# Two input quadrants kept on chip, transposed by columns, and projected by rows from there

## What is computed

```python
def layer_0(z):                                   # z is [256, 256, 64]
    n = ln(z)
    a = (n @ W_ap + b_ap) * sigmoid(n @ W_ag + b_ag) * mask[..., None]
    b = (n @ W_bp + b_bp) * sigmoid(n @ W_bg + b_bg) * mask[..., None]
    return z + einsum('ikc,kjc->ijc', a, b) @ W_z + b_z

def layer_1(x):
    n = ln(x)
    left  = sigmoid(n @ left1)  * (n @ left2)
    right = sigmoid(n @ right1) * (n @ right2)
    p = ln(einsum('sre,kre->ske', left, right))
    return x + (p @ out_w) * sigmoid(n @ gate)
```

## Time and profile before

| | us |
|---|---|
| median of 3 runs | 995.39 (992.37 to 997.83) |
| the profiled execution | 993.22 |
| its span | 991.6 |
| TensorE matmul busy | 817.9 |
| VectorE busy | 763.9 |
| ScalarE busy | 635.0 |
| GpSimd busy | 590.0 |

### The profile page before, as it was taken

How to read it: one execution, slowest core, us unless ns; L and a number is a source line. 1 busy time by engine, 2 the same in 40 slices (tenths; PEclk the granted TensorE clock), 3 DMA queues, 4 the chain that set the end, 5 groups by cost and what they waited for, 6 DMA issues and landing times.

```text
span 991.6 us, 26391 instructions
## 1 busy us (share of the span) xinstructions
PE 817.9 (82%) x9820; PEld 786.3 (79%) x9820; DVE 763.9 (77%) x1851; ACT 635.0 (64%) x866; POOL 590.0 (59%) x410
## 2 busy tenths in 40 slices
PE   4654444567999899989899999999999999999865
PEld 3553344467899799989899999898999898989754
DVE  6899999987589958995388888708980897069896
ACT  5698888765667536753266777547763776257664
POOL 7699999987256504660376444405661667068887
PEclk9789999798999999999899999999999999999999
DMA  4455489988789718969665768857982797876675
GB/s 139 117 161 150 131 275 297 342 286 299 256 274 316 226 33 270 307 205 282 235 194 156 241 214 297 325 193 215 296 279 66 216 306 225 291 253 226 212 233 191
DMA packets 173397, 228.75 MB, mean 231 GB/s; under 512 B 11224, under 2 KB 109784, under 8 KB 171224
## 3 DMA queue, kind: packets, MB, share of 16 engines
q1 hardware_dynamic: 172408, 226.96, 71.7%
q10 hardware_dynamic: 864, 0.12, 0.1%
HBM read 134.76 MB, written 92.27 MB: 229 GB/s over the span
## 4 chain that ended last, share of the span: by engine, by line
PE 43%; DVE 20%; DMA 15%; issue 11%; POOL 4%; ACT 3%; SPq 3%; DVEq 0%; POOLq 0%; ACTq 0%
PE bank L1117 18%; PE ps_w L1151 6%; DVE stats L944 6%; PE bank L1097 6%; DMA xin<-in_x_dram 6%; PE bank L1098 5%; DVE split L988 3%; PE ps_t L1136 3%; DMA xt<-xt 3%; DVE xc L981 2%; DMA xin<-x 2%; PE ps_x L1162 2%; DVE var L951 2%; DVE xc L973 2%; DMA chunk<-xcol 2%
## 5 line engine op out<-in xcount | busy, mean ns | idle before, releaser
L660 POOL TENSOR_TENSOR rstd<-var,minus_half 128x8 f32<-128x8 f32 x192 | 343.8, 1791 | 321.4 <-DVE var L951 321.4
L1117 PE MATMUL bank<-rhs,lhs 128*128 128x128 f32 x1536 | 227.6, 281 | 13.5 <-DVE lhs L924 7.5
L1117 PEld LDWEIGHTS bank<-rhs,lhs 128*128 128x128 f32 x1536 | 200.2, 196 | 16.4 <-DVE lhs L924 8.2
L718 ACT ACTIVATE sig<-bank 128x512 f32<-128x512 f32 x256 | 152.0, 602 | 63.5 <-PE bank L1098 61.1
L745 ACT ACTIVATE xt<-ps_x 128x1024 bf16<-128x1024 bf16 x128 | 130.9, 1022 | 60.6 <-PE ps_x L1162 47.1
L1162 PE MATMUL ps_x<-ident_b,split 128*128 128x128 bf16 x1024 | 83.3, 227 | 95.8 <-DVE split L988 95.3
L1162 PEld LDWEIGHTS ps_x<-ident_b,split 128*128 128x128 bf16 x1024 | 67.1, 102 | 107.3 <-DVE split L988 106.0
L981 DVE TENSOR_TENSOR xc<-xc,rstd 128x504 f32<-128x504 f32 (+1 forms) x192 | 137.9, 718 | 16.1 <-POOL xc L674 13.9
L1097 PE MATMUL bank<-w_rhs,chunk 128*128 128x128 bf16 x1024 | 136.9, 228 | 6.5 <-DVE rhs L916 2.7
L1098 PE MATMUL bank<-w_rhs,chunk 128*128 128x128 bf16 x1024 | 136.0, 227 | 0.0
L1097 PE MATMUL bank<-w_lhs,chunk 128*128 128x128 bf16 x928 | 125.8, 227 | 9.4 <-DVE lhs L916 4.4
(11 more groups left out here) (114 smaller groups left out, 1592.3 us busy)
## 6 DMA issues: line engine op xcount, KB each, us to landing
chunk<-xt SPq DMA_DIRECT2D x90, 512.0 KB, 4.5
xt<-xt SPq DMA_DIRECT2D x80, 512.0 KB, 5.4
xin<-in_x_dram SPq DMA_DIRECT2D x128, 256.0 KB, 4.7
x<-xin SPq DMA_DIRECT2D x64, 256.0 KB, 5.1
xin<-x SPq DMA_DIRECT2D x64, 256.0 KB, 4.9
out_dram<-xin SPq DMA_DIRECT2D x64, 256.0 KB, 4.6
spill<-lhs SPq DMA_DIRECT2D x8, 1024.0 KB, 5.4
chunk<-xcol SPq DMA_DIRECT2D x16, 512.0 KB, 5.6
```

The lines of the kernel that those rows point to most:

```text
L660: g.tensor_tensor(rstd[:, m % 2], var[:, m % 2], minus_half[:, :], ALU.pow).then_inc(rooted, 1)
L718: a.activation(sig[:, s], v[:, 0:C, :], ACT.Sigmoid).then_inc(gated, 1)
L1117: last = mm(bank[:, n], operand_of(q // 4, "lhs", kh)[:, c, :], operand["rhs"][:, kh, c, :], start=kh == 0, stop=kh == HALVES - 1)
```

## The change

Chunks 16 to 31 are no longer stored by rows and loaded back. `col_out` keeps quadrant 0 whole in the second half of the left operand's tile (`resident[0]`) and quadrant 2 whole in `quad` (`resident[2]`), 32 KB a partition each, and `project` reads a row of them as 128 elements that lie 128 bfloat16 (256 bytes) apart, where a row chunk has them 16 (32 bytes) apart. `xt_out` and `store_xt` are left out for quadrants 0 and 2; quadrant 2's columns are stored in 8 DMAs of 512 KB (`store_resident`) where there were 16 of 256 KB. Quadrant 3's first eight steps are staged in `chunk`. The schedule has three "last z" ticks where it had six, and steps 51 to 55 stand in the "second half" ticks; contraction 0 starts at tick 59 instead of 62. GpSimd's masks stay at their tick numbers, so those of ticks 59 to 61 now stand in the contraction's first three units, and a unit waits for its own channels' mask only. The spills move with them. At the start the seven `loads` stand in tick 1 and the six `loads_diag` in tick 3, behind the loads of steps 4 and 5. The diff, cut to its core:

```diff
     return layer, op, kind, half, i % GROUPS, i // GROUPS
-DIRECT = CHUNKS
+DIRECT = 2 * CHUNKS
...
         tick("z", m, [m])
-    for m in range(3 * STEPS, Z_LATE - 2):
+    for m in range(3 * STEPS, Z_HALF):
         tick("last z", m)
+    late = dict(zip((0, 2, 3, 5, 6), range(Z_HALF, Z_LATE)))
     for i in range(8):
-        tick("second half", {2: Z_LATE - 2, 5: Z_LATE - 1}.get(i), [48 + 2 * i, 49 + 2 * i], spill=(0, 0, i // 2 - 1) if i in (3, 5, 7) else None)
+        tick("second half", late.get(i), [48 + 2 * i, 49 + 2 * i], spill={5: (0, 0, 0), 7: (0, 0, 1)}.get(i))
     contraction(0, dict(zip((0, 1, 2, 3, 5, 6, 8, 9), range(Z_LATE, 4 * STEPS))),
-                {0: (0, 0, 3), 3: (0, 1, 0), 7: (0, 1, 1), 11: (0, 1, 2), 15: (0, 1, 3)})
+                {1: (0, 0, 2), 2: (0, 0, 3), 4: (0, 1, 0), 7: (0, 1, 1), 11: (0, 1, 2), 15: (0, 1, 3)})
...
     return ticks
-Z_EARLY, Z_LATE = 22, 56
+Z_EARLY, Z_HALF, Z_LATE = 22, 51, 56
...
 VECTOR_MASKS = {0: ("lhs", 1, 2), 1: ("lhs", 0, 2), 2: ("rhs", 0, 2)}
-EARLY = range(DIRECT + GROUPS, DIRECT + GROUPS + 6)
+def by_rows(m):
+    return step(m)[0] == "x" or step(m)[1] == 1
 def load_tick(n):
-    layer, _, kind, half, group, other = chunk_of(FIRST_OF[n])
-    last = 2 * STEPS + STEPS - 1 if n in EARLY else 0
-    if kind == "row":
-        last = STEPS * (QUADRANTS.index(("z" if layer == 0 else "x", half, other)) + 1) - 1
-    else:
-        last = X_BASE - 1
-    stored = TICK_OF[("store", "step", last)]
-    if n in EARLY:
-        return stored + (n - EARLY[0]) // 2
+    stored = TICK_OF[("store", "step", STEPS * (source_of(n) + 1) - 1)]
+    if n < DIRECT + 2:
+        return max(stored, TICK_OF[("store", "step", Z_LATE - 1)])
...
             at[0] += width
-            assert at[0] <= 6144
+            assert at[0] <= P * C
             return scratch[0:rows, at[0] - width:at[0]]
-        staged = [scratch[:, 6144 + 512 * n:6144 + 512 * (n + 1)].bitcast(BF16) for n in range(4)]
+        resident = {0: operand["lhs"][:, 1].rearrange("p c j -> p (c j)").bitcast(BF16),
+                    2: scratch.bitcast(BF16)}
...
         def col_buffer(m):
-            if m < 2 * STEPS:
+            q, c0 = m // STEPS, step(m)[3]
+            if q in resident:
+                return resident[q][:, P * c0:P * (c0 + COLS)]
+            if m < SIG_STAGED:
                 return chunk[:, (m // 2) % 2, P * COLS * (m % 2):P * COLS * (m % 2 + 1)]
-            if m < SIG_STAGED:
-                return staged[m % 4]
             return sig_staged[m % 2]
-        early = [scratch[:, 1024 * n:1024 * (n + 1)].bitcast(BF16) for n in range(len(EARLY))]
...
                 layer, _, kind, half, group, other = chunk_of(FIRST_OF[n])
-                if n in EARLY:
-                    sp.wait_ge(ready, 2)
-                    dst, landed = early[n - EARLY[0]], early_landed[n - EARLY[0]]
+                dst, landed = chunk[:, n % 2], chunk_landed[n % 2]
+                if n < DIRECT + 2:
+                    sp.wait_ge(projected, after(2 * CHUNKS - 1))
+                    for b in range(4):
+                        sp.wait_ge(col_stored[b], 16 * (Z_LATE - 3 * STEPS) // 4)
...
+            def store_resident(m):
+                _, rh, _, c0 = step(m)
+                sp.wait_ge(col_done, after(m))
+                sp.dma_start(xcol_dram[rh, :, c0 - COLS:c0 + COLS, :],
+                             resident[2][:, P * (c0 - COLS):P * (c0 + COLS)].rearrange("p (j r) -> p j r", r=P)
+                             ).then_inc(resident_stored, 16)
...
                 sp.dma_start(dst, src).then_inc(first_loaded, 16)
-            for dst, src in loads:
-                sp.dma_start(dst, src).then_inc(loaded, 16)
-            sp.wait_ge(zeroed, 1)
-            for dst, src in loads_diag:
-                sp.dma_start(dst, src).then_inc(loaded, 16)
...
                         load_x(m)
+                if t == 1:
+                    for dst, src in loads:
+                        sp.dma_start(dst, src).then_inc(loaded, 16)
+                if t == 3:
+                    sp.wait_ge(zeroed, 1)
+                    for dst, src in loads_diag:
+                        sp.dma_start(dst, src).then_inc(loaded, 16)
...
                 for m in due("store", t, "zx"):
-                    if m % 2:
+                    if m % 2 and by_rows(m):
                         store_xt(m)
-                    if 2 * STEPS <= m < X_BASE:
+                    if m % 2 and m // STEPS == 2:
+                        store_resident(m)
+                    if m // STEPS == 3:
...
             def col_out(m):
+                q = m // STEPS
                 act.wait_ge(x_turned, after(m))
-                if m < 2 * STEPS:
+                if q == 1 and m - 4 >= STEPS:
                     act.wait_ge(projected, after(m - 4))
-                elif m < SIG_STAGED:
-                    if m == 2 * STEPS:
-                        act.wait_ge(ready, 2)
-                    if m - 4 >= 2 * STEPS:
-                        act.wait_ge(col_stored[m % 4], 16 * ((m - 4 - 2 * STEPS) // 4 + 1))
-                else:
+                if m == 2 * STEPS:
+                    act.wait_ge(ready, 2)
+                if q == 3 and m < SIG_STAGED:
+                    if m - 4 < 3 * STEPS:
+                        act.wait_ge(projected, after(2 * CHUNKS - 1))
+                    else:
+                        act.wait_ge(col_stored[m % 4], 16 * ((m - 4 - 3 * STEPS) // 4 + 1))
+                if m >= SIG_STAGED:
...
                     if m - 2 >= SIG_STAGED:
-                        act.wait_ge(col_stored[(m - 2) % 4], 16 * ((m - 2 - 2 * STEPS) // 4 + 1))
+                        act.wait_ge(col_stored[(m - 2) % 4], 16 * ((m - 2 - 3 * STEPS) // 4 + 1))
...
                 if e == 0:
-                    for b in range(4):
-                        act.wait_ge(col_stored[b], 16 * (SIG_STAGED - 2 * STEPS) // 4)
+                    act.wait_ge(resident_stored, 16 * STEPS // 2)
...
                 for m in due("xt", t):
-                    xt_out(m)
+                    if by_rows(m):
+                        xt_out(m)
...
                     pe.wait_ge(ready, 1)
-                if k < DIRECT:
+                if k < CHUNKS:
                     pe.wait_ge(col_done, after(h))
-                    buf = chunk[:, k % 2]
+                    buf = resident[0][:, P * GRP * k:P * GRP * (k + 1)] if k < GROUPS else chunk[:, k % 2]
+                elif k < DIRECT:
+                    pe.wait_ge(col_done, after(STEPS * (2 * other + 1) - 1))
+                    buf = resident[2 * other]
...
                     n = LOAD_OF[k]
-                    if n in EARLY:
-                        pe.wait_ge(early_landed[n - EARLY[0]], 16)
-                        buf = early[n - EARLY[0]]
-                    else:
-                        pe.wait_ge(chunk_landed[n % 2], 16 * ring_uses(n))
-                        buf = chunk[:, n % 2]
+                    pe.wait_ge(chunk_landed[n % 2], 16 * ring_uses(n))
+                    buf = chunk[:, n % 2]
...
                     vec = COLS * s + n
-                    if kind == "row":
+                    if CHUNKS <= k < DIRECT:
+                        x_vec = buf.rearrange("p (j r) -> p j r", r=P)[:, :, GRP * group + vec]
+                    elif kind == "row":
...
                     pe.wait_ge(made, after(2 * NEEDS[q] - 1))
-                if q == 0 and u == 0:
-                    pe.wait_ge(masked_p, POOL_MASKS)
+                if q == 0:
+                    pe.wait_ge(masked_p, 2 * C // 4 + u + 1)
```

More of the change, by code:

```diff
@@ L74 @@
 FIRST_OF = {}
-LAST_OF = {_k: _k for _k in range(DIRECT)}
+LAST_OF = {}
 for _k in range(DIRECT, K_END):
@@ L211, with rows_through, source_of @@
 VECTOR_MASKS = {0: ("lhs", 1, 2), 1: ("lhs", 0, 2), 2: ("rhs", 0, 2)}
-EARLY = range(DIRECT + GROUPS, DIRECT + GROUPS + 6)
 def ring_before(n):
-    return n - 8 if n in (DIRECT + 14, DIRECT + 15) else n - 2
+    return n - 2
 def ring_uses(n):
-    return (n - DIRECT) // 2 + 1 - (3 if n >= DIRECT + 14 else 0)
-def load_tick(n):
-    layer, _, kind, half, group, other = chunk_of(FIRST_OF[n])
-    last = 2 * STEPS + STEPS - 1 if n in EARLY else 0
-    if kind == "row":
-        last = STEPS * (QUADRANTS.index(("z" if layer == 0 else "x", half, other)) + 1) - 1
-    else:
-        last = X_BASE - 1
-    stored = TICK_OF[("store", "step", last)]
-    if n in EARLY:
-        return stored + (n - EARLY[0]) // 2
+    return (n - DIRECT) // 2 + 1
+def by_rows(m):
+    return step(m)[0] == "x" or step(m)[1] == 1
+def rows_through(m):
+    return sum(by_rows(n) for n in range(m + 1))
+def source_of(n):
+    layer, _, kind, half, _, other = chunk_of(FIRST_OF[n])
+    rh, ch = (half, other) if kind == "row" else (other, half)
+    return QUADRANTS.index(("z" if layer == 0 else "x", rh, ch))
+def load_tick(n):
+    stored = TICK_OF[("store", "step", STEPS * (source_of(n) + 1) - 1)]
+    if n < DIRECT + 2:
```

(21 more changed lines are left out.)

16 lines of the change are left out of this document (8 added, 8 removed).

## The result

| us | before | after |
|---|---|---|
| median of 4 runs each | 996.61 (992.37 to 998.50) | 1049.43 (1048.42 to 1049.92) |
| ratio, 95% interval | | 1.0535 (1.0498 to 1.0572) |
| the profiled execution, its span | 993.22, 991.6 | 1049.78, 1047.7 |

The page of the kernel after: busy times, the granted clock in 40 slices of 26.2 us, the two DMA groups that changed.

A forecast was written before the change was run, and what follows sets the result against it. No engine is busy throughout; VectorE sets the tick to 181 us, then waits in ticks 51 to 61 with GpSimd as full. Gains 1.6 + 1.4 + 1.2 + 0.9 = 5.1 us give 990.3 us on the median's scale, range 984 to 998.

The forecast's parts named there:

- reading rows from columns: 512 matmuls loading weights 256 bytes apart instead of 32: taken as 0, bounds 0 to 1.0 us a half.
- the float32 row: Float32 transposes from `lhs` at 256 bytes, four in 0.80 us against 0.61 packed: upper bound 0.063 us a load.
- the rival of the strided loads: Sixteen halves 1.0 us dearer where TensorE then sets the ticks, some 5 us lost: 995.4 us; chance 0.08.
- The start: Moved weight loads let step 4's bn_stats go without a wait, its root near 17.0: 1.4 us earlier.
- Steps 34 to 51: DMA load about halves, so the pace falls from 3.46 to 3.37 us a step: 1.6 us gained.
- Step 51's bn_stats to root 59: Ticks 51 to 58 and first units, by GpSimd's queue: 52.2 us against 53.4, a gain of 1.2 us.
- The rest of contraction 0: After root 59, the late first fill's wait ends long before: 0.9 us gained, the rest unchanged.
- The masks' rival: Ticks 59 to 61: masks become contraction 0's bound, 8.9 us slower, 1004.3; decides over 62.3 us; chance 0.12.
- the sign of the masks: Root 59 more than 57 us after step 51's bn_stats would show the masks in the way.
- the 80 named: Matmuls over 0.08 us apart, listed as a sign of the forecast being wrong; 0.063 us was expected.

The follow-up runs named there:

- m64_256: The changed kernel with halves 32 to 63 loading 64 elements 256 bytes apart instead of 128, half of each result left out; 997.12 us, one execution.
- before_f32: The kernel before, with the 192 float32 transposes of `quad` reading 128 elements 256 bytes apart instead of packed; 995.48 us, one execution.
- the packed kernel: The changed kernel with halves 32 to 63 loading 128 packed elements (2 bytes apart) instead of 256 bytes apart, so other values; 994.39 us, ratio 0.9988 to before.
- stride32: The changed kernel with halves 32 to 63 reading the same tiles at 32 bytes' stride instead of 256, so other values; 994.93 us, ratio 1.0011 to before.

## Why the prediction was wrong

Forecast: 990.3 us, range 984 to 998. Measured 1049.43. The step that failed is **reading rows from columns**, costed at 0 with bounds of 0 to 1.0 us a half.

- *TensorE's own price* was near the upper bound: 121 ns between matmuls and not 63, 16 x 0.058 = 0.93 us a half, where the float32 row had given 1.0. I took 0, since 32 bytes seemed as scattered as 256. The row nearest in distance was that float32 one, and it said otherwise. The Trainium skill (SBUF — State Buffer, Door 1: The DMA port swizzle), by whose lines of 16 bytes both should cost the same, doesn't hold for this load: 148 ns against 258, and 240 bytes 146.
- *What this would cost* was the real error. The bounds asked what TensorE pays, and the rival of the strided loads asked when TensorE is no longer hidden. For TensorE's own time that rival had place and price right: m64_256 loses 5.0 us there, in the ticks with two halves, and nothing in the others. But VectorE, ScalarE and GpSimd paid far more, since their instructions advance at a fraction of their pace during the loads. The whole is 55.0 us over 32 halves (1.7 us each); the some 50 us of it that the other engines pay were in no term, bound or rival, and so the range missed by 51 us.
- No row of the kernel before could size it, but it left a bound unset: the argument took an engine's work beside TensorE for undisturbed. The one place to look was ScalarE beside the float32 loads at 256 bytes; its sigmoids take 611 ns there and 597 elsewhere, so it would have told me that nobody is held, and before_f32 shows the same. The form of the load, and not the distance alone, would have been missed.

The other terms, held against the packed kernel:

- *The start*: right. Step 4's bn_stats without a wait and its root at 16.98 us (forecast near 17.0), 1.4 us earlier. Step 25 comes 3.4 us earlier in the kernel after and 4.4 us packed, but 1.5 in stride32, with the same start. TensorE's granted clock there differs between executions (0.68 packed, 0.52 in stride32, 33 to 47 us), and I take no more than the 1.4 for the change.
- *Steps 34 to 51*: right in kind, 3.41 us a step in the mean (forecast 3.37, before 3.46), 0.9 us of the 1.6. Every step takes 3.37 us but the one of 4.10 that waits for its data.
- *Step 51's bn_stats to root 59*: 52.6 us (forecast 52.2, before 53.4).
- *The rest of contraction 0*: wrong in sign. From root 59 to half 64 it took 38.6 us, 4.7 more than before, where 0.9 less was forecast. ScalarE's wait before the first fill was gone, but I had counted the masks on GpSimd alone and not SyncE behind the spill that waits for them, nor its wait for the staged columns. The kernel before repeats its 33.9 us in before_f32, which is the same up to there. The sum of the packed kernel's stages, 5.1 us in the forecast, is 1.4 + 0.9 + 0.8 - 4.7 = -1.6 us at half 64. In its profile half 64 is 1.4 us early, but 3.0 us of that came before step 25, where executions differ, and the median shows nothing. So even without the harm of the strided loads the time would have been near 994 and not 990.3: inside the range, but by the range's width and not by the sum.
- *The masks' rival* had the place right and the point wrong: root 59 came far below its 62.3 us without the strided loads. In the kernel after it came 79.8 us after step 51's bn_stats, over the 57 us that I had named as the sign of the masks; it was the loads, and the matmuls 121 ns apart, over the 80 named, were the sign that told the two apart.

## What to carry to other kernels

A weight load with a stride can cost the other engines more than TensorE: before rows are read out of kept columns, look at the distance in bytes, and if it is 256 put some bytes between the columns (260 bytes: all but 0.4 of the 5.4% back). If all engines become slower at the same number of instructions, look first at what runs beside the slow ones in one tick of the timeline. And when work moves, follow the queue whose entries wait for it: here six masks cost little on their engine and more through the loads that stood behind a spill. A mean over many steps can hide one long one: list the steps before you look for a slower pace.

## What the runs showed of the hardware

- Loads of 128 bfloat16 columns took 98, 148, 203, 146, 258 and 157 ns with elements 2, 32, 128, 240, 256 and 260 bytes apart. I had expected one figure from 32 bytes on.
- Beside the 256-byte loads all three other engines slowed: mask 1.27 to 2.83 us, ScalarE's copy 1.02 to 2.21, VectorE's product 0.67 to 2.28 (medians of the packed and the changed kernel, steps 34 to 50), although the copy reads PSUM and only writes the tiles' memory. The Trainium skill (SBUF — State Buffer, Who interferes with whom) names the ports shared by VectorE and GpSimd as the only place where engines meet, and says that ScalarE never waits on anyone; these runs show TensorE's loads in the way of three engines.
- The clock fell to its lower level after the first slow half, in a window in which TensorE had 0.01 of 1.50 us of work, and was back at 0.8 and more only after the slow halves were over (the 5s in PEclk). At 2, 32, 128 and 240 bytes it is 1.00 throughout 134 to 181 us.
